# Group norm, 12-head attention and displaced convolution: VectorE adds the eighth key tile in four of six head pairs, and the order around the additions moves

## What is computed

```
x = x + attention(group_norm(x))        # 12 heads of 64 channels
    q, k, v = split(tokens @ W_qkv.T)
    scores  = var(v, over channels) @ var(k, over channels).T * 64**-0.5
    out     = softmax(scores) @ v
    out     = out @ W_proj.T + b_proj
x = x + displace(group_norm(x))         # per 16 channels: a shift, then a 3 x 3 kernel with zero padding
```

## Time and profile before

| | |
|---|---|
| median of three runs | 2211.66 us (2207.8 to 2215.89) |
| the profiled execution | 2203.28 us |
| its span, first to last instruction | 2201.7 us |
| mean granted TensorE clock | 0.965 of full speed |
| TensorE busy | 2016.2 us (92%) |
| VectorE busy | 1674.7 us (76%) |
| ScalarE busy | 1172.8 us (53%) |
| GpSimd busy | 157.6 us (7%) |
| share of the chain that ended last | TensorE 74%, VectorE 9%, DMA 7%, ACT 4% |

### The profile page before, as it was taken

The page is one execution under the profiler, slowest core; times in us unless marked ns, Lnnn a source line. Parts: engine busy times, 40 slices in busy tenths (PEclk is TensorE's granted clock), DMA queues, the critical chain, the costliest instruction groups (busy, mean ns, idle before and its releaser), DMA issues.

```text
span 2201.7 us, 36306 instructions
## 1 busy us (share of the span) xinstructions
PE 2016.2 (92%) x13036; PEld 1114.0 (51%) x13036; DVE 1674.7 (76%) x3695; ACT 1172.8 (53%) x1285; POOL 157.6 (7%) x215
## 2 busy tenths in 40 slices
PE   3999899989999899998999979998999989999970
PEld 2765257643666337562475525754366533765230
DVE  7677567887688875987778976788668887688738
ACT  5466625664266743667336752566427674266701
POOL 2000000010000000100000100000000110011101
PEclk8999999999999999999999989999999999999995
DMA  6412302344033511335122440234313351133304
GB/s 231 157 43 59 97 11 88 117 135 126 13 103 109 186 57 40 106 120 169 31 69 98 144 146 12 97 107 147 115 33 102 99 183 49 42 115 116 115 20 172
DMA packets 106985, 219.10 MB, mean 100 GB/s; under 512 B 53025, under 2 KB 53793, under 8 KB 106785
## 3 DMA queue, kind: packets, MB, share of 16 engines
q1 hardware_dynamic: 74816, 100.12, 15.6%
q0 software_dynamic: 25920, 94.38, 12.0%
q10 hardware_dynamic: 6048, 22.02, 2.8%
HBM read 158.28 MB, written 57.80 MB: 98 GB/s over the span
## 4 chain that ended last, share of the span: by engine, by line
PE 74%; DVE 9%; DMA 7%; ACT 4%; issue 3%; SPq 2%; POOL 1%; ACTq 0%; DVEq 0%; POOLq 0%
PE ps L1092 29%; PE ps L1131 25%; PE ps L1146 14%; PE ps L1113 4%; ACT ring L597 3%; DMA dt_sb<-d_sb 3%; DVE bt L800 2%; SPq L400 1%; DVE st L749 1%; DMA bt<-r_rows 1%; DMA cs_rows_y<-mv_y 1%; PE ps L1106 1%; DMA xv<-in_L_conv_W_qkv 1%; POOL ring L530 1%; DVE h_sp L740 0%
## 5 line engine op out<-in xcount | busy, mean ns | idle before, releaser
L597 ACT ACTIVATE ring<-a_sb,coef 128x1024 f32<-128x1024 f32 x768 | 809.9, 1137 | 53.9 <-PE ps L1131 53.3
L1092 PE MATMUL ps<-wkv_hi,h_sp 128*128 128x256 f16 x4608 | 776.3, 274 | 13.3 <-DVE h_sp L740 11.2
L1131 PE MATMUL ps<-ring,xv 128*64 128x512 f32 x3072 | 709.1, 608 | 0.0
L1092 PE MATMUL ps<-wkv_lo,h_sp 128*128 128x256 f16 x2304 | 630.1, 273 | 0.0
L1092 PEld LDWEIGHTS ps<-wkv_hi,h_sp 128*128 128x128 f16 x4608 | 451.9, 98 | 119.1 <-issue 50.0
L800 DVE TENSOR_TENSOR bt<-bt,ring 128x1024 f32<-128x1024 f32 x416 | 488.5, 1215 | 2.1 <-ACT ring L597 2.1
L1131 PEld LDWEIGHTS ps<-ring,xv 128*64 128x64 f32 x3072 | 209.7, 139 | 408.5 <-issue 388.7
L581 ACT ACTIVATE xv<-ps 128x256 f32<-128x256 f32 x192 | 73.4, 382 | 612.1 <-DVE st L749 612.1
L1146 PE MATMUL ps<-xv,wp_hi 128*128 128x512 f16 x1152 | 351.1, 383 | 18.3 <-issue 11.9
L749 DVE BATCH_NORM_STATS2 st<-ps 128x6 f32<-128x64 f32 x1536 | 217.8, 213 | 98.7 <-PE ps L1092 97.8
L1092 PEld LDWEIGHTS ps<-wkv_lo,h_sp 128*128 128x128 f16 x2304 | 225.9, 98 | 26.4
(11 more groups left out here) (122 smaller groups left out, 1305.2 us busy)
## 6 DMA issues: line engine op xcount, KB each, us to landing
a_sb<-a_rows SPq DMA_DIRECT2D x96, 512.0 KB, 6.1
xv<-in_x POOLq DMA_DIRECT2D x48, 512.0 KB, 3.6
bt<-r_rows SPq DMA_DIRECT2D x96, 256.0 KB, 4.0
h_sp<-in_x ACTq DMA_DIRECT2D x42, 512.0 KB, 4.4
shift_rows<-bt POOLq DMA_DIRECT2D x42, 512.0 KB, 6.4
out<-xv POOLq DMA_DIRECT2D x42, 512.0 KB, 3.5
shift_rows<-ring SPq DMA_DIRECT2D x12, 528.0 KB, 14.9
xv<-in_L_conv_W_qkv SPq DMA_DIRECT2D x4, 1152.0 KB, 9.1
```

The source lines that it names most:

```text
L597: nc.scalar.activation(ring_of(p, s, m), a_sb[:, h % 4, :], ACT.Exp, scale=coef[:, h, m:m + 1]).then_inc(s_exp, 1)
L1092: last = nc.tensor.matmul(ps[:, kv_bank[u % 2], half * 2 * P:(half + 1) * 2 * P], h_sp[:, k, hp, m * P:(m + 1) * P], wkv[wpart][:, k, q * ...
L1131: last = nc.tensor.matmul(ps[s * HD:(s + 1) * HD, o_bank[p % 2] + j, :], v_sb[:, p, m, s * HD:(s + 1) * HD], ring_of(p, s, m)[:, j * HALF: ...
```

## The change

It has four parts. (1) MD becomes (8, 8, 8, 8, 5, 5): in pairs 0 to 3 VectorE adds tile 7 too, and TensorE multiplies no tile of `ring` by ones. (2) The matmuls on the accumulators (`column_sums`) of pairs 0 to 2 stand behind the first key unit of the next pair, those of pair 3 behind the weighing of m = 0 of pair 4. (3) VectorE in pairs 1 to 4: the first head's additions 1 to 3 come first, then the statistics, `k_max`, `taps_y` and `gn`, then the second head's additions 1 to 3; `d_reciprocal` stands behind the additions of m = 4 (it was at m = 2), `o_normalise` at m = 6 behind the variances (it was at m = 4). In pair 5 `o_normalise` stands at m = 6 too, where nothing new comes ahead of it. (4) ScalarE at m = 3: `middle_tap` and the first `v_evict` come ahead of `d_copy`. `stats_to_groups` is cut into two functions that run as before.

```diff
-        MD = (7, 7, 7, 7, 5, 5)
+        MD = (8, 8, 8, 8, 5, 5)
...
+        def add_order(p):
+            m_of = ((1, 2, 3), (4,), (5,), (6,), (7,)) if 1 <= p <= 4 else [(m,) for m in range(1, MT)]
+            return [(s, m) for ms in m_of for s in (0, 1) for m in ms if m < MD[p]]
+
         def add_count(p, s, m):
-            return ADDS_TO[p] + 2 * (max(m, 1) - 1) + s + 1
+            return ADDS_TO[p] + add_order(p).index((s, max(m, 1))) + 1
...
                         if m == 3:
-                            if p:
-                                d_copy(b, p - 1, later)
                             if later:
                                 middle_tap(l1, p)
                             if p <= 3:
                                 v_evict(b, nxt)
+                            if p:
+                                d_copy(b, p - 1, later)
+                            if p <= 3:
                                 v_evict(b, nxt + 1)
...
+                    if 1 <= p <= 4:
+                        for m in (1, 2, 3):
+                            add_one(b, p, 0, m, later)
+                        if p <= 3:
+                            kv_stats(b, nxt)
+                        if p == 4:
+                            k_max(b, p + 1, later)
+                        if later:
+                            taps_y(l1, p, g_t, t_t)
+                            gn(l1, p + 1, g_t)
+                        if p <= 3:
+                            kv_stats(b, nxt + 1)
+                            k_max(b, p + 1, later)
+                        for m in (1, 2, 3):
+                            add_one(b, p, 1, m, later)
                     for m in range(MT):
-                        add_up(b, p, m, later)
-                        if m == 2:
-                            if p:
+                        if m and m < MD[p] and (m > 3 or p in (0, 5)):
+                            add_one(b, p, 0, m, later)
+                            add_one(b, p, 1, m, later)
+                        if p in (0, 5):
+                            if m == 2 and p == 5:
                                 d_reciprocal(b, p - 1)
...
+                        elif m == 4:
+                            d_reciprocal(b, p - 1)
+                        if m == 4 and p <= 4:
+                            k_scales(b, p + 1)
                         if m == 5 and p <= 3:
                             kv_stats(b, nxt + 2)
                         if m == 6:
                             if p <= 3:
                                 kv_stats(b, nxt + 3)
                                 variances(b, p + 2)
+                            if p:
+                                o_normalise(b, p - 1)
                             if later:
                                 taps_x(l1, p, t_t)
...
+            def column_sums(b, p, later):
+                pe.wait_ge(s_acc, b * NADD + ADDS_TO[p + 1])
+                if MD[p] == MT and (later or p):
+                    pe.wait_ge(s_dsb, b * NP + p)
+                denominators([acc_of(p, s) for s in (0, 1)], MD[p] == MT, True).then_inc(s_d, 1)
...
                         if m in (0, 4) and p <= 3:
                             kv_unit(b, nxt + m // 2, later)
+                            if m == 0 and p:
+                                column_sums(b, p - 1, later)
                             kv_unit(b, nxt + m // 2 + 1, later)
...
+                        if (p, m) == (4, 1):
+                            column_sums(b, p - 1, later)
                         weigh(b, p, m, later)
...
-                    pe.wait_ge(s_acc, b * NADD + ADDS_TO[p + 1])
-                    denominators([acc_of(p, s) for s in (0, 1)], False, True).then_inc(s_d, 1)
+                    if MD[p] < MT:
+                        column_sums(b, p, later)
```

More of the change, by code:

```diff
@@ L784, in k_scales, with add_one @@
                                         ALU.mult, ALU.min).then_inc(s_coef, 1)
[L786 to L800 removed]
+            def add_one(b, p, s, m, later):
+                i = (p * MT + m) * 2 + s
+                if m == 1:
+                    if s and (later or p):
+                        dve.wait_ge(s_d, b * NP + p)
+                    one = ring_of(p, s, 0)
+                else:
+                    dve.wait_ge(s_acc, b * NADD + add_count(p, s, m - 1))
+                    one = acc_of(p, s)
+                dve.wait_ge(s_exp, b * NT + i + 1)
+                nc.vector.tensor_tensor(acc_of(p, s), one, ring_of(p, s, m), ALU.add).then_inc(s_acc, 1)
             def d_reciprocal(b, p):
@@ L893, in span @@
+                    for m in range(MT):
+                        if m and m < MD[p] and (m > 3 or p in (0, 5)):
[3 more added lines that the diff above has]
+                            if m == 2 and p == 5:
                                 d_reciprocal(b, p - 1)
[L894 removed]
+                            if m == 2 and p == 0:
                                 kv_stats(b, nxt)
[L896 to L904 removed]
@@ L905, in span @@
-                        if m == 4:
-                            if p <= 4:
-                                k_scales(b, p + 1)
-                            if p:
-                                o_normalise(b, p - 1)
+                            if m == 3:
+                                if p == 0:
+                                    kv_stats(b, nxt + 1)
+                                    k_max(b, p + 1, later)
+                                if later:
+                                    taps_y(l1, p, g_t, t_t)
+                                    if p == 0:
+                                        gn(l1, p + 1, g_t)
+                        elif m == 4:
+                            d_reciprocal(b, p - 1)
```

30 lines of the change are left out of this document (5 added, 25 removed).

## The result

The changed kernel takes 2234.95 us (median of four runs, 2232.43 to 2243.27); the kernel before took 2210.57 beside it (four runs, 2207.8 to 2215.89). The ratio is 1.0113, 95% interval 1.0094 to 1.0132: 24 us slower, where 20 were predicted. The profiled execution took 2232.43 us (span 2230.9), 29 more than the profiled one before.

The account below looks back on a forecast made before the run. TensorE was taken to set the pace in pairs 0 to 3, then a chain VectorE, ScalarE, TensorE. First image -3, six at +2.9, last +5 gave +20 us on the median 2211.66: 2232 us, range 2203 to 2252.

Parts of the forecast that it names:

- the late reciprocal of pair 3: Pair 4, VectorE: it starts at 1017.5 instead of 1011.81, making m = 3 of pair 5 2.2 us later; chance 0.60.
- the signs that the prediction named: Ring group at 384 records, 576 additions, o_normalises 32.8 us apart, a 5 us gap ahead of pair 5, clock 0.5 behind.
- the walk: One image followed step by step from pair 0 into pair 5, where m = 3 is done at 1039.0 instead of 1036.8.
- the sum: First image -3 us, six images at +2.9, last image +5: together +19 to +21, say +20 us.
- The loop: From one o_normalise to the next through ScalarE's exponentials and VectorE: 32.8 us, longer than a pair took before.
- ScalarE's leg: From o_normalise through o_first, add_bias, evictions and the seventh exponential to the first head's third addition: 11.3 us.
- VectorE's bill: Pairs 0 to 3: two more additions take 2.26 us, raising VectorE's work from 29.8 to 32.1 us a pair.
- The saving of TensorE: Pairs 0 to 3: four eighth-tile matmuls go, 0.88 us a pair, 28 us over eight images if TensorE sets the time.
- The clock: Behind the new gap ahead of pair 5 TensorE runs at 0.50 of full speed, costing 0.7 us an image.
- TensorE keeps the pace: Rival: if pair 3's reciprocal starts by about 1015, 3.5 us an image are kept, -28, 2184 us; chance 0.15.
- Nothing to measure: Rival: loss in pair 4 and gain in pairs 0 to 3 cancel, 2205 to 2218 us; chance 0.13.
- The sums come late on TensorE: Rival: late last additions hold column_sums and stall TensorE in every image, +16 on top, 2248 us; chance 0.12.

Follow-up runs that it names:

- e1: The changed kernel with, in pair 4 alone, the reciprocal of pair 3 moved ahead of the second head's additions; 2212.64 us.
- e11: The changed kernel with 36 matmuls that nobody reads in TensorE's idle time ahead of pair 5; 2247.36 us, ratio 1.0174.
- e6: The changed kernel with d_reciprocal directly behind k_max and o_normalise at m = 5 in pairs 1 to 4, eight tiles kept; 2187.15 us.
- e12: The kernel of e6 with, in pair 4, the second head's three additions ahead of taps_y and gn; 2174.66 us, ratio 0.9839.
- e14: The kernel of e12 with the first six additions of pairs 1 to 3 alternating between the heads; 2259.24 us, ratio 1.0236.
- e7: The kernel of e6 with MD = (7, 7, 7, 7, 5, 5) and the sums at the pair's end; 2188.78 us.
- e13: The kernel of e12 with MD = (8, 8, 8, 7, 5, 5), pair 3's eighth tile back on TensorE; 2168.22 us, ratio 0.9816.
- e15: The kernel of e12 with MD = (7, 7, 7, 7, 5, 5) and the sums at each pair's end; 2170.57 us, ratio 0.9841.
- e5: The kernel before with MD = (8, 8, 8, 8, 5, 5) alone, order kept, sums at the pair's end; 2222.76 us, ratio 1.0054.
- e3: The kernel before with k_max, in pair 4 alone, behind the additions of m = 1, ahead of the reciprocal; 2192.22 us, ratio 0.9928.
- e4: The changed kernel's order with MD back at (7, 7, 7, 7, 5, 5) and sums at the pair's end; 2244.05 us, ratio 1.0165.
- e8: The kernel of e3 with pair 5's key scales sent first in pair 4, o_first(3) and add_bias(3) behind pair 5's first two exponentials; 2194.44 us.

## Why the prediction was right, and where not

**The sign and the main cause** are right, and shown: the late reciprocal of pair 3. Moving it alone (e1) takes 22 us back, and the signs that the prediction named all came: 576 additions on VectorE where there were 512, 384 ones-matmuls on `ring`, the gap of 5 us ahead of pair 5 and the clock of 0.50 behind it. Each step of the walk, from `o_normalise`(2) on: reciprocal at +22.8, measured +23.15; `o_normalise`(3) 7.5 to 8.5 behind it, measured 8.11; TensorE's wait ahead of pair 5 some 5 us, measured 5.04; first projection at +44.3, measured +46.04 (1048.10). The last is 1.7 late: 0.35 from the reciprocal, 0.1 from the transfers, 0.6 since the exponentials start 3.84 behind `o_normalise`(3), not 3.27, because they wait 0.48 for `a_sb`, whose broadcast stands behind `r_broadcast` in SP's queue. The walk had no line for that queue. Of the other 0.7, 0.5 is the slow clock behind the gap (e11), which the sum had booked apart, and 0.14 the exponentials, which take 8.55 us for 8.41. Ahead of this stretch the walk was 1.9 us early in this image: it had `o_normalise`(2) 194.8 us behind the last reciprocal of the image before (994.7 - 799.9), measured 196.7 (1002.06 - 805.34). TensorE's gain up to pair 4 was put at 3.6 us and is 2.6 on average.

**What the walk did not have** are the two gaps inside pair 4, 2.64 and 3.15 us, and the low clock behind them. It let TensorE run from pair 4 to the gap ahead of pair 5. While the late reciprocal holds pair 5 they should cost little more, since TensorE would wait there instead (not tried by itself); once it is early, gaps of this kind are what is left (3.60 and 1.54 us in e1, 4.49 in e6, which e12 takes down).

**The loop** was put at 32.8 us and measures 33.03: ScalarE's leg 11.19 for 11.3, VectorE's 21.84 for 21.5.

**VectorE's bill** is the step that came out wrong: "29.8 us of work, with its own issue gaps. With the two that the change adds it is 32.1." It is 32.88 (e6). I took the distance of additions from alternating pairs of them, 1.13 us, while the change lines up three on one accumulator. These start 1.33 apart (e14 puts 0.56 us a pair on it; the rest is not told apart). It did no harm to the forecast, since the loop of 33.03 stood above it. But from 32.1 it followed that, with VectorE only busy, TensorE's saving would be kept. It is not so. Without the loop the kernel does win (e6, 22 us), but as much with seven tiles as with eight: in e6 VectorE lags 1.1 us a pair, and pair 4 gives TensorE's saving back (e6 against e7).

**The saving of TensorE** stands where it should: 640 ones-matmuls became 384, their busy time 85.2 became 51.1 us, and weighings stand 31.75 us apart in e6. Nothing of it reached the end in e7 against e6, and little in e13 against e15.

**The clock**: 0.7 us an image in the sum, 0.47 measured beside the stretch in e11. The granted clock is 0.50 behind the gap and 1.00 without it; the Trainium skill (TensorE: Matmul & The Clock Gate, HAM oscillation), by which waits between bursts bring it down, agrees with this. The forecast had the price small because the exponentials pace the weighings there, and that is so ahead of pair 5. Inside pair 4 it is not: behind the gap of 2.64 us eight records take 1.3 us more. In the whole run the weighings are busy 18.4 us longer, 2.3 an image, where the forecast had 0.7 for the clock.

**The sum**: first image -3, measured -2.8; six images at +2.9, measured +3.6; last image +5, measured +9.7, twice as much. There TensorE comes to pair 4 no sooner than before (201.3 us behind the image before, 201.4 in the kernel before), so nothing stands against the 9.7 us that it loses from there to pair 5's first projection (42.2 for 32.5); why the lead is missing was not tried. In all +20 against +24 by the medians and +29 by the profiled executions.

**The rivals.** *TensorE keeps the pace* asked for a reciprocal 2.5 us earlier than the walk and then 2184 us. In e1 it was 5.5 earlier than in the walk (17.33 behind `o_normalise`(2) for 22.8) and the kernel took 2212.64: the condition was met, and the time was not. Part of that is the transfers, which took 3.4 us more, and the gaps in pair 4. But the rival's 28 us did not follow from its condition either: by the walk's own steps a reciprocal 2.5 us earlier puts the first projection at 1036.5, where it was 1036.8 before, and so leaves the kernel about as fast as before. That is what e1 shows. The rule of the Trainium skill (Perfetto Trace Analysis, Identifying the Most-Contended Engine), to optimise the engine with the highest occupancy first, gave nothing here when it was taken as taking work off TensorE: 2222.76 us against 2208.4 in the old order (e5), and no clear difference in the mended one (e6 and e7, e12 and e15). *Nothing to measure* (2205 to 2218 us) is excluded by the time. *The sums come late on TensorE* did not appear: in the changed kernel TensorE's list of waits has none for an addition. It does in e6, with 12.8 us in seven waits.

## What to carry to other kernels

When the busiest engine is relieved, look first at the place where it already waits; here most of the result was decided in one pair of six, by how early a reciprocal starts whose answer must travel through memory before anyone can use it. In these runs the instruction that starts such a trip was worth more ahead of the work that merely fills time, even where its data cost a short wait (0.20 us in e1, 1.27 in e6). And a stall that is removed shows up again in part at the next dependence: 7.50 us taken away gave 2 us an image on average (e3, 16 us over eight), so the gain is worth walking to the end of the chain before it is booked.

## What was not expected of the hardware

- Additions of 128x1024 in a row on one accumulator start 1.33 us apart, on two accumulators by turns 1.14 (VectorE's timelines of the changed kernel and of e14). An addition is 1.22 us long in both.
- The same trip from the reciprocal to `o_normalise`(3), a small write and the broadcasts, took 8.11 us in the changed kernel, 8.39 in e11, 8.73 in e4, 11.05 in e8 and 11.56 in e1, each time with VectorE waiting for its end. In e8 two broadcasts of 512 KB had been issued ahead of it. In e1 the next image's loads and the shifted window were issued within 4.4 us of it, and its broadcasts took 9.8 us from their issue (4.8 in the changed kernel); that these slow it down is likely, but was not tested.
- Thirty-six matmuls in otherwise idle time brought the clock back up, from 0.50 to 1.00 in that stretch, and the kernel was still 12 us slower. Why is open.
- The granted clock was 0.58 and 0.61 behind waits of 2.64 and 3.15 us in the changed kernel, and 0.57 a microsecond behind one of 1.95 us in e6, but 1.00 behind one of 2.66 us in e11. So here the length of a wait did not tell by itself whether the clock fell.
